# A context projection begun in the softmax tail, and the end of a linear attention with its last key chains on VectorE

## The chip, the cores and the metric

The kernel runs on one core of a Trainium2 chip. The metric is the device time of one execution in microseconds, the median of several runs.

## The reference

The input x is 4 batches of 512 tokens with 256 channels, in float32. Four residual steps follow each other, each on a layer norm of x:

```python
x = x + attn_a(layernorm(x))   # 16 heads of 16 channels, softmax over 512 keys, then ctx @ Wproj.T + bproj
x = x + ffn(layernorm(x))      # router over 8 experts, top 2; silu(silu(xr @ w1.T) @ w3.T) @ w2.T
x = x + attn_b(layernorm(x))   # 16 heads of 128: conv of 4 taps, silu, norm of q and k; S = (1-b) S + b v k'; o = S q, times gate, @ Wo
x = x + ffn(layernorm(x))
```

The expert step adds all its gated rows to the first 8 rows of x (`out.at[indices].add`), so that only a sum per expert and a small tail come after the two hidden layers.

## The kernel before

Tokens lie on the partitions in `x_tok` (16 tiles of 128 tokens). Matmuls in full precision are made of three passes with operands split into a high and a low part: ScalarE copies a bank of PSUM into the high part, VectorE subtracts it from the bank for the low part, and TensorE multiplies high x high, high x low, low x high. Each engine has its own program, and the order of all four is written out by hand; semaphores join them. A stage is a block, and at the end of a block every engine waits for all others.

The first attention goes over 8 groups (4 batches, two halves of the channels) in slots: 8 slots (chunks) for a group, 64 in all, and a lag of 6. A slot holds the row maxima of the group in hand (TensorE scores, VectorE `tensor_reduce`, L698), and the transposed scores, exponentials and context of the chunk 6 slots earlier (L441, L617, L457). So slots 64 to 69, the tail, have no maxima. Every fourth chunk a context of four head slots is copied (L624), transposed (L402) and divided by its sum into 16 columns of `ctx_tok` (L716, L718); this is done 16 times, and the 16th stands at the end of the stage, behind the last context. Scores use three banks in turn, and the context of chunk n-1 waits for all four exponentials of that chunk. In slot 66 the scores also wait for a DMA that puts the last maxima into the operands.

`project_context` (L777) is a block of its own behind it. For each batch it transposes `ctx_tok` (L799, 8 transposes), makes the high and low parts (L834, L850), multiplies with both halves of the contraction (L822, 24 matmuls in two halves) and adds to `x_tok` (L863). It also makes the high and low parts of two weights (L828, L854, L836, L870), and on the way the norm of the first group for the next stage: statistics (L83, L86), deviations on GpSimd (L96, L98), normalise (L106), transposes (L130), parts (L116, L121).

`norm_and_ffn` (L878) runs over 4 groups of 4 tiles: router (L974), two halves of the upper layer (L994), transposes of the next norms (L130), middle layer (L1006). `begun` says how many norms were counted and done ahead. The stage behind the first attention begins with (2, 1), and its GpSimd splits the head weights meanwhile (L1151 to L1177); the last stage, behind the linear attention, begins with (3, 2).

`linear_attention` (L1185) goes through 64 units (8 pairs of heads, 4 batches, 2 heads) as a software pipeline with up to 6 units in flight: projections of q and k, conv on VectorE (L1804), transposes, statistics, scales on GpSimd (L1367 to L1381, a chain of ten small instructions), normalise on ScalarE (L1705), transposes back (L1511), affine (L1721), scores (L1496), mask (L1863), sums of chunks (L1563), carry of the state (L1822), reading it out (L1578, L1581), gate (L1869), high and low parts of the gated output (L1728, L1426 on GpSimd), projection out (L1595) and addition to `x_tok` (L1846). The key chain of a unit is three instructions on GpSimd (scale L1388, shift L1404, decay L1414), and the queries' decay is a fourth (L1397). `drain()` of each engine holds what is left of the units 58 to 63 (LAST = 63), and the norms of groups 0 and 1 for the last stage. A drain thus has one order per engine:

```python
score_unit(LAST - 1, BODY - 2)                  # TensorE, before
read_state(LAST - 2, BODY - 3, LAST - 4, 0)
turn_back(LAST, 0)
sum_chunks(LAST - 1, BODY - 2)
turn_back(LAST, 1)
score_unit(LAST, BODY - 1)
ln_d.transpose(pe, 0, proj)
```

`unread(bank, n)` (L422) is n matmuls of 128x512 whose result nobody reads.

## Time and profile before

| what | us |
|---|---|
| median of 3 runs | 1172.69 (1171.26 to 1176.45) |
| the profiled execution | 1177.77 |
| its span | 1176.0 |
| TensorE busy | 1127.3 (96%) |
| VectorE busy | 932.3 (79%) |
| ScalarE busy | 773.7 (66%) |
| GpSimd busy | 635.6 (54%) |

The mean granted TensorE clock was 0.983 of full speed (2.4 GHz); where it is 0.50 the engine runs at 1.2 GHz. Rows of a timeline give start, duration, engine, line and operation; "x8" merges eight instructions. In brackets stands the idle time before the row, and what ended it. PE is TensorE, DVE is VectorE, ACT is ScalarE, POOL is GpSimd; a "q" behind a name is an engine's sequencer, which stands there where a block ended.

### The profile page before, as it was taken

The page shows a single profiled execution, that of the slowest core. Times are in us where ns is not written, and L with a number is a line of the kernel's source. Part 1 is how long each engine was busy: PE and PEld are TensorE (multiplying, and loading weights), DVE is VectorE, ACT ScalarE, POOL GpSimd, SP SyncE. Part 2 cuts the span into 40 slices and gives each one's busy share as a digit, 9 for nine tenths or more (in the row PEclk, how much of TensorE's full clock was granted, in tenths as well). Part 3 has the DMA queues.
Part 4 walks back from the last instruction along what each step waited for, and adds up shares of the span by engine and source line. Part 5 has one row for each costly group of instructions (what it writes and reads, how often), then busy time and mean ns, then how long its engine had stood idle before and what let it go on. Part 6 is the DMA issues. An engine that isn't in the chain of part 4 may idle for free. (4 is left out here: it accounts for less than half of the span.)

```text
span 1176.0 us, 22452 instructions
## 1 busy us (share of the span) xinstructions
PE 1127.3 (96%) x7559; PEld 907.9 (77%) x7559; DVE 932.3 (79%) x2126; ACT 773.7 (66%) x1535; POOL 635.6 (54%) x1077
## 2 busy tenths in 40 slices
PE   8999999987998899999999999999999999999788
PEld 7444434336666799999999999999999999999776
DVE  6988887836558888888888888888888888888762
ACT  3477677762447676767676777777777777676533
POOL 4020500000705777786777686777687777767630
PEclk9999999987999999999999999999999999999899
DMA  6333333300320112102111211211211211010020
GB/s 184 55 55 56 55 55 56 55 2 2 115 70 20 35 48 68 48 33 77 40 48 33 84 33 48 68 48 34 80 37 39 78 33 47 33 48 33 32 72 1
DMA packets 23449, 60.50 MB, mean 51 GB/s; under 512 B 3367, under 2 KB 8359, under 8 KB 22183
## 3 DMA queue, kind: packets, MB, share of 16 engines
q1 hardware_dynamic: 23335, 59.07, 18.8%
q8 instruction: 61, 1.00, 0.4%
q14 instruction: 53, 0.43, 0.1%
HBM read 44.67 MB, written 2.33 MB: 40 GB/s over the span
## 5 line engine op out<-in xcount | busy, mean ns | idle before, releaser
L1804 DVE SCALAR_TENSOR_TENSOR ln_xn<-l_proj_q,par,ln_xn 128x511 f32<-128x511 f32 (+2 forms) x192 | 142.6, 743 | 98.0 <-ACT ln_xn L1688 95.6
L698 DVE TENSOR_REDUCE a_neg_max<-a_scores 128x1 f32<-128x512 f32 x244 | 154.9, 683 | 31.2 <-PE a_scores L419 29.4
L617 ACT ACTIVATE a_probs<-a_scores_t 128x512 f32<-128x512 f32 x256 | 138.3, 600 | 59.5 <-PE a_scores_t L441 58.4
L1694 ACT ACTIVATE ln_xn<-ln_xn,par 128x512 f32<-128x512 f32 x128 | 92.6, 723 | 93.3 <-DVE ln_xn L1804 93.3
L1388 POOL TENSOR_TENSOR l_k_tok<-l_normed,k_norm 128x384 f32<-128x384 f32 x64 | 65.0, 1016 | 153.8 <-ACT l_normed L1705 151.9
L1804 DVE SCALAR_TENSOR_TENSOR ln_xn<-l_proj_k,par,ln_xn 128x511 f32<-128x511 f32 (+2 forms) x192 | 143.2, 746 | 4.5
L1705 ACT ACTIVATE l_normed<-l_turn_q,l_shift,l_scale 128x128 f32<-128x128 f32 x252 | 94.8, 457 | 22.3 <-POOL l_shift L1381 22.3
L1379 POOL TENSOR_TENSOR l_scale<-l_small,l_minus_half 128x8 f32<-128x8 f32 x64 | 105.0, 1641 | 5.0
L1705 ACT ACTIVATE l_normed<-l_turn_k,l_shift,l_scale 128x128 f32<-128x128 f32 x252 | 95.6, 480 | 0.0
L1762 ACT ACTIVATE l_gate<-l_proj_gv 128x512 f32<-128x512 f32 x64 | 38.2, 597 | 79.1 <-PE l_proj_gv L1476 79.1
L1578 PE MATMUL l_outp<-l_masked,l_values 128*128 128x128 f32 x512 | 88.6, 275 | 1.0 <-issue 1.0
L1811 DVE TENSOR_TENSOR_SCAN l_decay<-l_keep,ident 128x128 f32<-128x128 f32 x256 | 87.1, 403 | 0.0
L1426 POOL TENSOR_TENSOR l_gated_lo<-l_gated,l_gated_hi 128x512 fp32r<-128x512 f32 x64 | 83.1, 1299 | 5.1 <-ACT l_gated_hi L1728 5.1
L96 POOL TENSOR_SCALAR ln_var_eps<-ln_mean_var 128x4 f32<-128x4 f32 (+1 forms) x13 | 3.0, 230 | 148.4 <-DVE ln_mean_var L79 89.9
L441 PE MATMUL a_scores_t<-a_stack 50*128 50x512 f32 x256 | 74.9, 497 | 7.3 <-ACT a_probs L617 5.2
L1489 PE MATMUL l_proj_gv<-head_hi,xn_hi 128*128 128x256 f32 x256 | 76.5, 299 | 0.3 <-ACT l_gate L1762 0.3
L441 PEld LDWEIGHTS a_scores_t<-a_stack 50*128 50x128 f32 x256 | 28.9, 186 | 61.6 <-ACT a_probs L617 40.7
L1581 PE MATMUL l_outp<-l_q_late,l_state 128*128 128x128 f32 x384 | 74.2, 275 | 0.0
L89 POOL MEMSET ln_minus_half<- 128x4 f32 (+1 forms) x4 | 0.4, 100 | 136.1 <-POOLq L171 136.1
L1578 PEld LDWEIGHTS l_outp<-l_masked,l_values 128*128 128x128 f32 x512 | 72.6, 192 | 1.1 <-issue 1.1
L457 PE MATMUL a_ctx_acc<-a_probs,a_v_tok 128*32 128x512 f32 x512 | 70.8, 626 | 2.3 <-ACT a_probs L617 1.7
L1496 PEld LDWEIGHTS l_scores<-l_qk 128*128 128x128 f32 x512 | 67.5, 193 | 6.2 <-ACT l_qk L1721 1.3
(369 smaller groups left out, 3622.7 us busy)
## 6 DMA issues: line engine op xcount, KB each, us to landing
l_keep<-keep_rows SPq DMA_DIRECT2D x64, 448.0 KB, 3.5
a_stack<-a_dense SPq DMA_DIRECT2D x90, 128.0 KB, 4.3
head_raw<-w_heads SPq DMA_DIRECT2D x8, 1024.0 KB, 6.7
x_tok<-x SPq DMA_DIRECT2D x4, 512.0 KB, 8.3
wo_raw<-w_o SPq DMA_DIRECT2D x1, 2048.0 KB, 11.4
out<-x_tok SPq DMA_DIRECT2D x1, 1920.0 KB
a_stack<-a_max_rows_t SPq DMA_DIRECT2D x64, 4.0 KB
ctx_tok<-w_qkv SPq DMA_DIRECT2D x1, 768.0 KB, 6.8
```

What stands on the lines that cost most here:

```text
L441: pe.matmul(scores_t[q % TURNS][:], half_rows(k_stack[i], e, STACK + 2)[:, slot, t * P:(t + 1) * P], half_rows(q_stack[i], e, STACK + 2)[: ...
L617: act.activation(probs[:, n % 2, h, :], scores_t[(4 * n + h) % TURNS][:], ACT.Exp, scale=SOFT_SCALE).then_inc(probs_done, 1)
L698: dve.tensor_reduce(neg_max[:, g % 2, at:at + 1], max_bank(g, j), AX.X, ALU.max, negate=True).then_inc(max_done, 1)
L1379: pool.tensor_tensor(scale[:, i, :], small[:, 7, :], minus_half[:], ALU.pow).then_inc(scales_ready, 1)
L1426: pool.tensor_tensor(gated_lo[:, k % 4, :], gated[:], f32(gated_hi[:, k % 4, :]), ALU.subtract).then_inc(gated_lo_done, 1)
L1489: last = pe.matmul(proj_gv[:, t * PAIR:(t + 1) * PAIR], lhs, rhs, start=(j == 0), stop=(j == 3 * KD - 1))
L1578: last = pe.matmul(outp[:, tok], values[:, c % 2, t, e * DK:(e + 1) * DK], masked[:, m, tok], start=True, stop=(t == 0))
L1581: last = pe.matmul(outp[:, tok], state[:, m, t - 1, :], q_late[:, m, (t - 1) * P:t * P], start=False, stop=True)
L1694: act.activation(conv[:, w, m, :], conv[:, w, m, :], ACT.Silu, bias=par[:, h, 2 * TAPS + w:2 * TAPS + w + 1]).then_inc(act_sem[w], 1)
L1705: last = act.activation(normed[:, w, t, :], turn_bank(v, w)[:, t * P:(t + 1) * P], ACT.Identity, scale=scale[:, m, j:j + 1], bias=shift[:, ...
L1804: ins = dve.scalar_tensor_tensor(conv[:, w, m, s:], proj[w][:, 0:SEQ - s], par[:, h, tap:tap + 1], conv[:, w, m, s:], ALU.mult, ALU.add)
L1811: last = dve.tensor_tensor_scan(decay[:, tok], keep[:, r, tok], ident[:], 0.0, ALU.mult, ALU.add)
```

## The change

1. `project_context` is gone. Its work is cut into 8 parts, one for a half of the contraction and a batch. Parts 0 to 3 (the channels of the first 8 contexts) are turned in slots 64 to 67 and multiplied in slots 65 to 68; parts 4 to 7 come behind the last context. All of parts 0 to 3 use one bank, `scores[0]`, for their transposes, and two banks take the products of all 8 parts; each part is added to `x_tok` by itself. The parts of `proj_w` are made in slots 60 and 61, those of `w_in` in slots 62 and 63. The operands lie in `dense`, so no memory is added. The norm of group 0 for the next stage is done behind part 6 as before.
2. In the tail and behind it are 22 `unread` matmuls (4, 3, 4, 5, 6), in the drain of the linear attention 10 (4, 2, 4), and 4 at the head of each expert stage (both of them).
3. In `norm_and_ffn`, if one norm was done ahead, the transposes of group 1 move behind the first half of the upper layer, their high parts behind its activation, and each group's low parts come ahead of the next group's normalise. The last stage now begins with (2, 1) too.
4. In the drain of the linear attention the key chains of units 62 and 63 (but for the scaling of 62's) and the queries' decays of both are on VectorE. Norm group 1 is counted there, but no longer normalised or turned. The order on each engine is new, and the banks of the last outputs are others, so that waits for `added` fall away. ScalarE's high part of unit 60 moves ahead of the normalise of unit 62.

The core of the diff:

```diff
+            def turn_part(n):
+
+                k, b = n // NB, n % NB
+                if n == 0:
+                    pe.wait_ge(max_done, groups * tiles_per_group)
+                elif n < NB or n == PARTS - 1:
+                    pe.wait_ge(p_lo_done, min(n, NB))
+                else:
+                    pe.wait_ge(probs_done, 4 * groups * chunks)
+                pe.wait_ge(ctx_done, groups * quads // KD * (k + 1))
+                for t in range(TPB):
+                    last = pe.transpose(part_banks[n][:, t * P:(t + 1) * P], ctx_tok[:, b, t, k * P:(k + 1) * P], ident[:])
+                last.then_inc(p_turned, 1)
+
+            def project_part(n):
+
+                k = n // NB
+                pe.wait_ge(p_lo_done, n + 1)
+                if n == 0:
+                    pe.wait_ge(p_w_lo_done, 1)
+                for half in range(2):
+                    if n >= 1:
+                        pe.wait_ge(p_added, 2 * n - 1 + half)
+                    for e in range(2):
+                        tok, j = slice((2 * half + e) * P, (2 * half + e + 1) * P), 0
+                        for lhs, rhs in split_passes(ctx_hi[n % 2][:, tok], ctx_lo[n % 2][:, tok], p_w_hi[:, k, :],
+                                                     p_w_lo[:, k, :]):
+                            last = pe.matmul(acc_banks[half][:, e * D:(e + 1) * D], lhs, rhs, start=(j == 0), stop=(j == 2))
+                            j += 1
+                    last.then_inc(p_acc_done, 1)
+
             pe.wait_ge(ident_ready, 1)
...
+                        if last_max <= slot < last_max + NB:
+                            turn_part(slot - last_max)
                     else:
                         if n < 0:
                             after_context(s, c)
                         after_scores(s, c)
+                        if last_max < slot <= last_max + NB:
+                            project_part(slot - last_max - 1)
+            pe.wait_ge(ctx_done, quads * groups - 1)
+            unread(misc, 4)
             context(groups * chunks - 1)
-            pe.wait_ge(ctx_done, quads * groups - 1)
+            unread(misc, 3)
             transpose_context(quads * groups - 1)
+            unread(ctx_acc, 4)
+            for n in range(NB, PARTS):
+                turn_part(n)
+            for n in range(NB, PARTS):
+                if n == PARTS - 1:
+                    ln_b.transpose(pe, 0, norm_banks)
+                project_part(n)
+                if n == NB + 1:
+                    unread(ctx_acc, 5)
+            unread(scores_t[0], 6)
...
+            def high_part(n):
+
+                act.wait_ge(p_turned, n + 1)
+                if n >= 2:
+                    act.wait_ge(p_acc_done, 2 * (n - 1))
+                act.activation(ctx_hi[n % 2], part_banks[n][:], ACT.Copy).then_inc(p_hi_done, 1)
...
+                if slot == last_max - 4:
+                    act.wait_ge(w_loaded, 16 * len(loads))
+                    for quad in range(quads):
+                        act.wait_ge(stacked[1][quad], copies(groups - 1, quad))
+                    act.activation(p_w_hi, proj_w[:], ACT.Copy).then_inc(p_w_hi_done, 1)
+                if slot == last_max - 2:
+                    act.activation(w_in_hi[:], w_in_raw[:], ACT.Copy).then_inc(w_in_hi_done, 1)
+                if last_max <= slot < last_max + NB:
+                    high_part(slot - last_max)
             copy_context(groups * quads - 1)
+            for n in range(NB, PARTS):
...
+            def add_part(n):
+
+                for half in range(2):
+                    at = n % NB * TPB + 2 * half
+                    dve.wait_ge(p_acc_done, 2 * n + half + 1)
+                    if n == 0 and half == 0:
+                        dve.wait_ge(bias_added, 1)
+                    if n >= NB and half == 0:
+                        dve.wait_ge(p_added, 2 * (n - NB + 1))
+                    dve.tensor_tensor(x_tok[:, at:at + 2, :], acc_banks[half][:].rearrange("p (t d) -> p t d", t=2),
+                                      x_tok[:, at:at + 2, :], ALU.add).then_inc(p_added, 1)
...
+                if last_max <= slot < last_max + NB:
+                    low_part(slot - last_max)
+            normalise(groups * quads - 1)
+            low_part(NB)
+            for n in range(NB, PARTS):
+                if n + 1 < PARTS:
+                    low_part(n + 1)
+                add_part(n)
+                if n == NB:
+                    dve.wait_ge(p_added, 2 * n + 2)
+                    ln_b.statistics(dve, 0)
+                elif n == NB + 1:
+                    ln_b.normalise(dve, 0)
+                elif n == NB + 2:
+                    dve.wait_ge(p_added, 2 * n)
+                    ln_b.statistics(dve, 1)
+            ln_b.low_parts(dve, 0, norm_banks)
...
             router(0)
-            if done < 2:
-                ln.transpose(pe, 1, xt)
             for g in range(NB + 1):
                 if g < NB:
                     if g + 1 == NB:
                         turn_logits(g)
-                    for m in range(KD):
-                        upper(g, m)
+                    upper(g, 0)
+                    if g == 0 and done < 2:
+                        ln.transpose(pe, 1, xt)
+                    upper(g, 1)
...
             for g in range(done, NB):
+                if g >= done + 1 and done < 2:
+                    ln.low_parts(dve, g - 1, xt)
                 ln.normalise(dve, g)
-                if g >= done + 1:
+                if g >= done + 1 and done >= 2:
                     ln.low_parts(dve, g - 1, xt)
                 if g - done + begin < NB:
                     ln.statistics(dve, g - done + begin)
...
             def drain():
-                rows_in = 16 * NB * PAIRS
                 gated_low(LAST - 3, BODY - 4)
                 scaled_keys(LAST - 1)
                 scales(LAST, BODY - 1)
                 ln_d.deviations(pool, 0)
-                decayed_queries(LAST - 1, BODY - 2, rows_in)
-                shifted_keys(LAST - 1)
-                decayed(LAST - 1, BODY - 2)
-                scaled_keys(LAST)
-                shifted_keys(LAST)
-                decayed(LAST, BODY - 1)
                 gated_low(LAST - 2, BODY - 3)
-                decayed_queries(LAST, BODY - 1, rows_in)
-                ln_d.deviations(pool, 1)
                 gated_low(LAST - 1, BODY - 2)
                 gated_low(LAST, BODY - 1)
-                ln_d.deviations(pool, 2)
+                ln_d.deviations(pool, 1)

...
                 wait(pe, values_done, UNITS)
                 project_out(LAST - 4, BODY - 5, head)
                 score_unit(LAST - 1, BODY - 2)
+                sum_chunks(LAST - 1, BODY - 2)
                 read_state(LAST - 2, BODY - 3, LAST - 4, 0)
                 turn_back(LAST, 0)
-                sum_chunks(LAST - 1, BODY - 2)
+                unread(proj_q, 4)
+                read_state(LAST - 1, BODY - 2, 0, LAST - 1)
                 turn_back(LAST, 1)
                 score_unit(LAST, BODY - 1)
-                ln_d.transpose(pe, 0, proj)
-                read_state(LAST - 1, BODY - 2, 0, LAST - 1)
+                unread(proj_q, 2)
                 sum_chunks(LAST, BODY - 1)
                 wait(pe, added, LAST - 3)
                 project_out(LAST - 3, BODY - 4, head)
                 read_state(LAST, BODY - 1, 0, LAST)
-                wait(pe, added, LAST - 2)
                 project_out(LAST - 2, BODY - 3, head)
-                ln_d.transpose(pe, 1, proj)
+                ln_d.transpose(pe, 0, proj)
                 wait(pe, masked_done, UNITS)
                 project_out(LAST - 1, BODY - 2, head)
-                wait(pe, added, LAST - 1)
                 project_out(LAST, BODY - 1, head)
+                unread(chunks, 4)
...
                     silu(pair, k, u, 1)
+                if u == LAST:
+                    gated_high(LAST - 3, BODY - 4)
...
+            def shifted_keys(v):
+                wide = [P, LATER, DK]
+                wait(dve, k_scaled, v + 1)
+                dve.tensor_tensor(k_tok[:], k_tok[:],
+                                  k_norm[:, 1, :].unsqueeze(1).to_broadcast(wide), ALU.add).then_inc(k_shifted, 1)
...
             def drain():
                 add_out(LAST - 5, BODY - 6)
                 token_statistics(LAST, BODY - 1)
+                shifted_keys(LAST - 1)
+                decayed_keys(LAST - 1)
+                decayed_queries(LAST - 1, BODY - 2)
+                mask(LAST - 1, BODY - 2)
+                carry(LAST - 1, BODY - 2)
+                decays(LAST, BODY - 1, 16 * NB * PAIRS)
+                gate_out(LAST - 2, BODY - 3)
+                add_out(LAST - 4, BODY - 5)
                 wait(dve, added, UNITS - BODY + 2)
                 ln_d.statistics(dve, 0)
-                mask(LAST - 1, BODY - 2)
-                gate_out(LAST - 2, BODY - 3)
+                scaled_keys(LAST)
+                shifted_keys(LAST)
+                decayed_keys(LAST)
+                mask(LAST, BODY - 1)
+                decayed_queries(LAST, BODY - 1)
+                gate_out(LAST - 1, BODY - 2)
+                carry(LAST, BODY - 1)
                 ln_d.normalise(dve, 0)
-                add_out(LAST - 4, BODY - 5)
-                decays(LAST, BODY - 1, 16 * NB * PAIRS)
-                carry(LAST - 1, BODY - 2)
-                mask(LAST, BODY - 1)
-                gate_out(LAST - 1, BODY - 2)
+                gate_out(LAST, BODY - 1)
+                add_out(LAST - 3, BODY - 4)
+                add_out(LAST - 2, BODY - 3)
                 wait(dve, added, UNITS - BODY + 4)
                 ln_d.statistics(dve, 1)
-                carry(LAST, BODY - 1)
-                add_out(LAST - 3, BODY - 4)
                 ln_d.low_parts(dve, 0, proj)
-                gate_out(LAST, BODY - 1)
-                ln_d.normalise(dve, 1)
-                add_out(LAST - 2, BODY - 3)
-                wait(dve, added, UNITS - BODY + 6)
-                ln_d.statistics(dve, 2)
-                ln_d.low_parts(dve, 1, proj)
                 add_out(LAST - 1, BODY - 2)
                 add_out(LAST, BODY - 1)
```

## Rows read from the trace of the kernel before

**Rows 1.** Windows: start:end, us, busy (count) of PE, PEld, DVE, ACT, POOL, PEclk, DMA, GB/s
```profile
250.00:254.00 4.00, 2.56 (x16) 0.90 (x14) 0.00 (x0) 3.09 (x6) 0.00 (x0) 1.00 0.00 1
254.00:258.00 4.00, 3.21 (x17) 1.02 (x20) 0.00 (x0) 3.15 (x8) 0.00 (x0) 0.74 0.00 0
258.00:262.00 4.00, 4.00 (x16) 1.34 (x12) 0.37 (x2) 1.64 (x4) 0.00 (x0) 0.50 0.00 0
294.00:296.00 2.00, 2.00 (x8) 1.29 (x7) 1.91 (x9) 0.59 (x1) 0.00 (x0) 0.50 0.87 283
1110.00:1112.00 2.00, 1.12 (x4) 0.72 (x4) 2.00 (x3) 1.41 (x5) 1.88 (x2) 0.50 0.00 0
```

**Rows 2.** TensorE's timeline in the softmax tail: start us, us, engine line op [idle before]
```profile
246.74 0.28 PE L396 MATMUL a_misc<-ident,a_max_parts 128*32 128x128 f32 x1
...
248.63 1.06 PE L457 MATMUL a_ctx_acc<-a_probs,a_v_tok 128*32 128x512 f32 x8
...
249.62 0.50 PE L441 MATMUL a_scores_t<-a_stack 50*128 50x512 f32 x2
...
266.05 1.94 PE L457 MATMUL a_ctx_acc<-a_probs,a_v_tok 128*32 128x512 f32 x8 [1.17 <-ACT a_probs L617]
```

**Rows 3.** ScalarE's timeline in the softmax tail
```profile
244.60 2.07 ACT L617 ACTIVATE a_probs<-a_scores_t 128x512 f32<-128x512 f32 x4 [0.65 <-PE a_scores_t L441]
```

**Rows 4.** VectorE's timeline at the end of the softmax tail
```profile
270.20 0.42 DVE L718 TENSOR_TENSOR ctx_tok<-a_misc,a_rden 128x256 f32<-128x256 f32 x1
```

**Rows 5.** TensorE's timeline in the projection's stage and behind it
```profile
276.76 0.28 PE L822 MATMUL p_acc<-p_w_hi,p_ctx_hi 128*128 128x256 f32 x1
...
278.56 1.03 PE L799 MATMUL p_turned<-ident,ctx_tok 128*128 128x128 f32 x8
...
292.93 0.40 PE L974 MATMUL f_sums_b<-xn_hi,w_in_hi 128*8 128x512 f32 x1 [2.25 <-PEq L779]
```

**Rows 6.** VectorE's timeline in the projection's stage
```profile
271.60 0.69 DVE L854 TENSOR_TENSOR p_w_lo<-proj_w,p_w_hi 128x512 fp32r<-128x512 f32 x1 [0.97 <-ACT p_w_hi L828]
...
279.48 1.41 DVE L83 BATCH_NORM_STATS2 ln_stats<-x_tok 128x6 f32<-128x256 f32 x4
...
282.25 1.28 DVE L863 TENSOR_TENSOR x_tok<-p_acc,x_tok 128x512 f32<-128x512 f32 x2
...
284.07 1.38 DVE L106 TENSOR_SCALAR ln_xn<-x_tok,ln_mean_var,ln_rstd 128x256 f32<-128x256 f32 x4
```

**Rows 7.** GpSimd's timeline in the projection's stage
```profile
281.65 1.04 POOL L98 TENSOR_TENSOR ln_rstd<-ln_var_eps,ln_minus_half 128x4 f32<-128x4 f32 x1
```

**Rows 8.** TensorE's timeline in the first expert stage
```profile
300.02 0.40 PE L974 MATMUL f_sums_b<-xn_hi,w_in_hi 128*8 128x512 f32 x1 [0.26 <-DVE xn_lo L121]
...
307.35 0.40 PE L974 MATMUL f_sums_b<-xn_hi,w_in_hi 128*8 128x512 f32 x1 [1.62 <-DVE xn_lo L121]
```

**Rows 9.** VectorE's timeline in the first expert stage
```profile
303.03 3.07 DVE L106 TENSOR_SCALAR ln_xn<-x_tok,ln_mean_var,ln_rstd 128x256 f32<-128x256 f32 x4 [1.47 <-POOL ln_rstd L98]
...
312.03 3.52 DVE L1094 TENSOR_TENSOR beta_lo<-beta_w,beta_hi 128x32 fp32r<-128x32 f32 x1
```

**Rows 10.** GpSimd's timeline in the first expert stage
```profile
311.90 3.61 POOL L1175 TENSOR_SCALAR wo_hi<-wo_raw 128x4096 fp32r<-128x4096 f32 x1
```

**Rows 11.** GpSimd's timeline in the linear attention's drain
```profile
1103.84 1.00 POOL L1388 TENSOR_TENSOR l_k_tok<-l_normed,k_norm 128x384 f32<-128x384 f32 x1
...
1106.56 1.64 POOL L1379 TENSOR_TENSOR l_scale<-l_small,l_minus_half 128x8 f32<-128x8 f32 x1
...
1128.10 1.35 POOL L1426 TENSOR_TENSOR l_gated_lo<-l_gated,l_gated_hi 128x512 fp32r<-128x512 f32 x1 [1.57 <-ACT l_gated_hi L1728]
```

**Rows 12.** ScalarE's timeline in the drain
```profile
1108.51 1.50 ACT L1705 ACTIVATE l_normed<-l_proj_q,l_shift,l_scale 128x128 f32<-128x128 f32 x4 [4.67 <-POOL l_shift L1381]
```

**Rows 13.** TensorE's timeline in the drain and behind it
```profile
1110.07 1.12 PE L1511 MATMUL l_turn_q<-ident,l_normed 128*128 128x128 f32 x4 [3.43 <-ACT l_normed L1705]
...
1134.61 0.39 PE L974 MATMUL f_sums_d<-xn_hi,w_in_hi 128*8 128x512 f32 x1 [1.69 <-PEq L1204]
```

160 lines of the change are left out of this document (58 added, 102 removed).

## The prediction

> **What bounds the kernel now.** I read the busy times first, then the windows of the span, then the timelines of the two places that the change touches. TensorE is busy for 96% of the span, so a gain must come from where it isn't, or where it is busy at half its clock. The windows show two such stretches. In the softmax tail it works for 2.56 of 4 us at 250 to 254, and then the granted clock goes from 1.00 to 0.74 to 0.50, that is from 2.4 to 1.2 GHz [rows 1]. The same matmuls of the context take 1.06 us at 248.6 and 1.94 us at 266.0 [rows 2]. Full clock is back at 276.8, in the middle of the projection, where a matmul of 256 columns follows the one before it by 0.12 us and eight transposes take 1.03 us [rows 5]. In the drain of the linear attention TensorE waits 3.43 us for ScalarE's normalise, which itself waited 4.67 us for GpSimd's scales [rows 12, 13], and it runs at 0.50 from there [rows 1]. After both the next stage starts late: the first router matmul stands at 292.93 with 2.25 us idle before it, and at 1134.61 with 1.69 us [rows 5, 13]. After the idle time of 2.25 us the clock fell again, 0.50 at 294 to 296 [rows 1].
>
> **Softmax tail, slots 64 to 69.** Before, from the last transpose of maxima at 246.74 to the end of the last context's division at 270.62 it is 23.9 us [rows 2, 4]. New work for TensorE in slots 65 to 67: two pairs of scores at 0.35 to 0.5, together 0.7, a context 1.0 from its start to that of the scores behind it [rows 2], four transposes 0.5, twelve matmuls at 0.12 make 1.4 [rows 5], together 3.6 us. ScalarE has four exponentials, 2.1 us [rows 3], and a high part of 0.6, so 2.7. But parts 0 to 3 share one bank, and so there is a ring: transposes 0.5, the slot's second pair of scores 0.5 to its first exponential, two exponentials 1.1, high part 0.6, low part 0.65, hand-overs 0.3, together 3.7 us, a little more than TensorE's own work. Slot 64 ends at 248.4, four slots of 3.7 make 263.2, slot 69 with scores and context 1.8 makes 265.0. Then the last exponentials, the context at full clock, the copy, transposes and the division: 1.8, 1.0, 0.7, 0.6 and 0.8, which makes 269.9. That is 0.7 us early. The 7 unread matmuls stand in the waits for the exponentials and the copy. The weights' parts in slots 60 to 63 are 1.3 us on ScalarE and 0.69 twice on VectorE [rows 6]; both have idle time there, so between 0 and 2.7 us; I take 0.6, for VectorE paces the maxima. Sum of the tail: about 0 (bounds: 2 us gained, 5 lost). The DMA of the maxima that slot 66 waits for is covered by the new work.
>
> **The projection behind the last context.** Before: 270.62 to 292.93, 22.3 us [rows 4, 5]. New, from the division's end: the block's end and the weights' first parts are gone. Four unread matmuls lie beside the division. First part turned at 0.6, high part 1.2, low part 1.9, products to 3.5. From there VectorE is the chain: adding 1.28 a part [rows 6], statistics 1.6 (1.41 begins, the aggregates follow), low parts 0.6 each, normalise 1.38 [rows 6], with GpSimd's 1.04 [rows 7] beside an addition. From 1.9: low part of 5 beside the products, first addition 2.9 to 4.2, statistics 5.8, low part 6.4, addition 7.6, normalise 9.0, low part 9.6, addition 10.8, statistics 12.4, addition 13.6, low parts of the norm 14.8, end of the block 15.1. TensorE has 16 transposes and 48 matmuls, half of before, and fits in. Gain 22.3 - 15.1 = 7.2; I take 7 (bounds 5 and 9).
>
> **The first expert stage.** Four unread matmuls cost 0.9 us, as nothing is waited for. Router(1) then waits for the low parts of group 1: 0.9 + 1.4 router + 1.4 upper + 0.9 transposes, high parts behind the activation and its table load, low parts: 6.9 us from the start, against 300.02 - 292.93 = 7.1 with a stretch at half clock [rows 8, 1]. Router(2) waited 1.62 us for low parts that stood behind a normalise of 3.07 us [rows 8, 9]; they now stand ahead of it, and this stall goes; late next are the transposes of group 3, by at most 0.5. Whether the clock falls is open: TensorE's gap is 2.2 us now as well. Held: 2.0 gained, fallen: 1.0. I take 1.5 (bounds 2 and -1).
>
> **The drain.** The time from the scales' end S (ScalarE's normalise begins, 1108.51 [rows 12]) to the router at 1134.61 [rows 13] is 26.1 us. New, in us after S and at full clock (where no row is named, the steps at the pace that they have in the 600 us of steady state before: turning back 0.5, scores 1.0, sum of chunks 0.7, reading the state 1.5, and 0.6 to 0.7 for an instruction of ScalarE or VectorE over 512 columns, as the additions' [rows 6]): normalise of q and k to 2.8 (1.4 each); turn back q 2.0, four unread 2.9, reading unit 62's state 4.5, turn back k 5.0, affine 5.9, scores 7.0, mask 7.7, queries 8.2, gate of 62 8.9, carry 9.5, with the sum of chunks to 8.2 and a projection out to 9.7 beside it; reading unit 63 to 11.2. VectorE's normalise stands ahead of the gate of 63 and meets GpSimd's low part, 2.3 instead of 1.4: 11.8, gate 12.5, high part 13.1, low part on GpSimd 1.35 [rows 11] to 14.5, two projections out at 24 x 0.12 to 17.4, last addition and unread 18.3, block's end 18.7. That is 7.4 less. The key chain of 63 on VectorE (3 x 0.55, from 0.69 for 512 columns and 0.42 for 256 [rows 6, 4], against 1.00 on GpSimd [rows 11]) ends at 5.2, before the scores, so it costs nothing; if the scores were not the later ones, it would cost 1.7. S itself: GpSimd's scales begin 1.0 us earlier, since unit 60's high and low parts came earlier, and end 0.3 to 1.0 earlier, but the three instructions for unit 62 on VectorE fall in the midst of them.
>
> A row decides what that costs. In the expert stage a VectorE subtraction of 128x32 with both inputs in SBUF took 3.52 us while GpSimd ran one instruction of 3.61 us [rows 9, 10], so the two don't run side by side. The Trainium skill, page "SBUF — State Buffer", section "SBUF: two separate sides", says the same as a rule: the pair of ports that both engines share is taken for a whole instruction by a VectorE operation with two inputs in SBUF against a GpSimd operation that reads SBUF. By that rule, as by the row, moving keys to VectorE is no free relief for the engine that makes the scales.
>
> By the row, the chain of scales is held up by 0 to 3 x 0.55 = 1.7 us; I take 0.8 and S unchanged. Then the last stage pays: four unread matmuls 0.9, the transposes of group 1 0.9, and a wait of 0.6 for their parts, 2.4. Drain and last stage: 7.4 - 0.5 (GpSimd held up beyond the early start) - 2.4 = 4.5 gained (bounds 7 gained, 1 lost).
>
> **Sum.** 0 + 7 + 1.5 + 4.5 = 13.0 us. The profiled execution took 1177.77 (span 1176.0 and 1.8 around it), so 1164.8 for it; it was 5.1 above the median of 1172.69. From the median: 1159.7. Within 0.5% is 5.9 us, about what a measurement can tell.
>
> **Rivals.** (a) The ring in the tail is slower than 3.7 us a slot: the high part stands behind the slot's exponentials, and each slot's scores wait for banks. For: ScalarE's exponentials often wait for scores in the tail, 0.65 us before one group [rows 3]. Against: all steps were counted. At 5.0 a slot it costs 4 x 1.3 = 5 us: 1165.
> (b) The drain gives nothing: GpSimd's scales wait for VectorE, TensorE is then idle for 2 to 2.5 us before the turn back of q, and its clock falls as it did behind 3.43 and 2.25 us of idle time, doubling some 4 us of work. For: those two rows [rows 5, 13]; against: 1.69 us of idle time brought no fall. 0.8 more for S and 4 for the clock: 1164.5.
> (c) Slower than before: the clock falls in slot 64 or 65 already and doesn't come back up to the end of the projection. Then 3.6 us of TensorE's work a slot becomes 7.2, four slots and a half give 16, and behind the last context some 4 more: 20 - 13 = 7 over, 1180. For: in this tail it did fall, and the projection's matmuls up to 276 ran at half [rows 1, 5]. Against: it fell behind a stretch with 1.4 of 4 us idle, which now has the parts in it. It decides from about 13 us of work at half clock on.
> (d) (a) and (b) together, or a covered stall in both, which ends within 0.5%: 1168.
>
> **Chances.** Forecast 0.58, (a) 0.13, (b) 0.13, (c) 0.06, (d) 0.10. The forecast's own range is 1155 to 1165; with (a), (b) and (d) 1154 to 1170. Faster by over 0.5% (under 1166.8): the forecast and nearly all of (a) and (b), 0.82; the same: (d) and the rest, 0.12; slower: 0.06.
>
> **What would show it.** Right: no block between the tail and the projection; granted clock near 1.00 from 246 to the first expert stage; slots 65 to 68 of 3.5 to 3.9 us; the last division near 270; from there to the router about 15; router(2) without a wait; the drain from S to the last stage's router about 19 us, and S within 1 us of before. Wrong: 0.50 in any window from 250 to 285, slots of over 4.5 us, ScalarE's normalise of unit 63 later than before relative to the last step, or the last stage longer by more than 3 us.

## The result, and the profile after

The changed kernel takes 1168.41 us (median of 13 runs, 1167.14 to 1170.89) against 1172.70 (13 runs, 1171.14 to 1179.90): ratio 0.996, 95% interval 0.9949 to 0.9972, so 4.3 us less by the medians, where 13.0 were forecast. The time lies outside the forecast's own range (1155 to 1165) and inside the one that takes in the rivals (1154 to 1170); the gain is a third of the forecast. The profiled execution took 1167.14, the lowest of the 13, and its span is 1165.3. Medians here and below leave out three runs in a slow state: two of the kernel before (1390.21 and 2754.50 us) and one of no_unread (1249.68).

The table splits the span of the two profiled executions at the points that the prediction used: the last transpose of maxima (slot 64), the last division, the next block's first matmul on TensorE, the linear attention's first, the scales' end S, and the last stage's first.

| stretch, us | before | after | difference | forecast |
|---|---|---|---|---|
| up to the transpose of slot 64 | 246.74 | 247.17 | +0.4 | 0 |
| tail, to the last division | 23.88 | 24.50 | +0.6 | 0 |
| projection, to the first expert stage | 22.31 | 15.48 | -6.8 | -7 |
| first expert stage | 41.67 | 39.95 | -1.7 | -1.5 |
| linear attention up to S | 773.91 | 773.65 | -0.3 | +0.5 |
| drain behind S | 26.10 | 20.66 | -5.4 | -7.4 |
| last stage | 41.39 | 43.89 | +2.5 | +2.4 |
| span | 1176.0 | 1165.3 | -10.7 | -13.0 |

By these two executions the forecast was 2.3 us off; by the medians it was 8.7 off. The profiled execution of before stands 5.1 us above its median and that of after 1.3 below, which are the 6.4 us between the two answers. The experiments must say where in the span they lie.

The windows of after (columns as in [rows 1]):

```profile
250.00:254.00 4.00, 3.85 (x32) 2.44 (x28) 1.22 (x2) 2.60 (x6) 0.00 (x0) 1.00 0.01 2
254.00:258.00 4.00, 4.00 (x32) 2.43 (x28) 1.33 (x3) 3.07 (x7) 0.00 (x0) 1.00 0.00 0
258.00:262.00 4.00, 4.00 (x32) 2.37 (x31) 2.30 (x4) 2.63 (x5) 0.00 (x0) 1.00 0.00 0
...
294.00:296.00 2.00, 1.89 (x11) 0.84 (x12) 2.00 (x8) 0.30 (x1) 0.00 (x0) 1.00 1.03 433
...
1104.00:1108.00 4.00, 3.49 (x20) 3.16 (x18) 1.36 (x3) 0.80 (x2) 1.14 (x1) 0.68 0.00 0
```

The clock stays at 1.00 through the tail, where it was 0.74 and 0.50 [rows 1], and TensorE is busy nearly all the time, not 2.56 of 4 us. At 294 it is 1.00 as well. In the drain it still falls, to 0.68.

One slot of TensorE's timeline in the tail of after, and ScalarE's exponentials in it:

```profile
249.50 1.07 PE L471 MATMUL a_ctx_acc<-a_probs,a_v_tok 128*32 128x512 f32 x8
250.72 0.66 PE L571 MATMUL a_scores<-ident,ctx_tok 128*128 128x128 f32 x4 [0.15 <-DVE a_dense L805]
251.30 0.50 PE L455 MATMUL a_scores_t<-a_stack 50*128 50x512 f32 x2
251.74 1.70 PE L587 MATMUL a_scores<-a_dense 128*128 128x256 f32 x12
...
253.79 1.06 PE L471 MATMUL a_ctx_acc<-a_probs,a_v_tok 128*32 128x512 f32 x8
```

```profile
251.83 1.09 ACT L678 ACTIVATE a_probs<-a_scores_t 128x512 f32<-128x512 f32 x2 [0.92 <-PE a_scores_t L455]
```

From context to context the slot takes 4.29 us, the next ones 4.07 (the contexts start at 257.86, 261.94 and 265.81). TensorE does not wait within it but for 0.15 us: context 1.0, transposes 0.58, scores 0.43 twice, twelve matmuls 1.63. It is ScalarE that waits, 0.92 us, for scores that stand behind the twelve matmuls.

VectorE from the last division on, and TensorE at the start of the first expert stage:

```profile
271.25 0.42 DVE L798 TENSOR_TENSOR ctx_tok<-a_misc,a_rden 128x256 f32<-128x256 f32 x1
...
278.50 1.28 DVE L816 TENSOR_TENSOR x_tok<-a_scores,x_tok 128x512 f32<-128x512 f32 x2
```

```profile
287.15 1.17 PE L1031 MATMUL f_up_b<-w_in_hi 128*128 128x512 f32 x4 [1.69 <-PEq L171]
...
294.11 0.39 PE L994 MATMUL f_sums_b<-xn_hi,w_in_hi 128*8 128x512 f32 x1 [0.77 <-DVE xn_lo L121]
...
299.63 0.39 PE L994 MATMUL f_sums_b<-xn_hi,w_in_hi 128*8 128x512 f32 x1
```

The additions take 1.28 us, the statistics 1.40 and the normalise 1.37, as before [rows 6]. The router of group 1 comes 6.96 us after the start of the stage, that of group 2 without the wait of 1.62 us [rows 8].

The drain of after on ScalarE, TensorE and VectorE:

```profile
1100.75 1.51 ACT L1724 ACTIVATE l_normed<-l_proj_q,l_shift,l_scale 128x128 f32<-128x128 f32 x4 [2.23 <-POOL l_shift L1405]
```

```profile
1097.30 0.91 PE L1578 MATMUL l_chunks<-l_values,l_k_tok 128*128 128x128 f32 x6 [0.15 <-issue]
...
1102.31 0.66 PE L1526 MATMUL l_turn_q<-ident,l_normed 128*128 128x128 f32 x4 [2.54 <-ACT l_normed L1724]
1102.72 1.71 PE L1667 MATMUL l_proj_q<-wo_hi 128*128 128x512 f32 x4
...
1121.41 1.16 PE L1031 MATMUL f_up_d<-w_in_hi 128*128 128x512 f32 x4 [0.30 <-PEq L1228]
```

```profile
1111.98 2.36 DVE L106 TENSOR_SCALAR ln_xn<-x_tok,ln_mean_var,ln_rstd 128x256 f32<-128x256 f32 x4
```

ScalarE's wait for the scales is 2.23 us instead of 4.67 [rows 12], but not because the scales come earlier: the copy of unit 62's state, 0.28 us at 1098.24, now stands in the midst of it and itself waits 2.59 us. TensorE waits 2.54 us instead of 3.43 [rows 13], since the sum of unit 62's chunks (1097.30) now stands ahead of S. Even so the clock falls behind this wait: the four unread matmuls behind the turn back of q take 1.51 us up to the next row at 1104.23, and reading unit 62's state 2.66, up to 1106.89.

S itself comes later. The last conv instruction of VectorE ends 10.6 to 10.7 us before S in the four profiled executions with the old drain, and 11.3 to 11.4 us before it in the eight with the new one. What differs between them on VectorE is the scans of the decays, in before and in after:

```profile
1100.26 1.36 DVE L1811 TENSOR_TENSOR_SCAN l_decay<-l_keep,ident 128x128 f32<-128x128 f32 x4
```

```profile
1091.81 2.11 DVE L1830 TENSOR_TENSOR_SCAN l_decay<-l_keep,ident 128x128 f32<-128x128 f32 x4
```

In after, GpSimd's low part of unit 60 runs from 1091.40 to 1092.69, earlier than before, and the scans that begin beside it take 0.75 us longer. VectorE's normalise at 1111.98 takes 2.36 us beside GpSimd's low part (1112.17 to 1113.55); 2.3 were assumed.

### The profile page after: what moved, and what is told of

Read it like the earlier page. It is cut to its first block and busy times, and to the rows that moved or that the text cites. A ratio compares the mean times of both kernels' runs of the same rounds, so it can differ in the third digit from the quotient of the medians.

```text
span 1165.3 us, 22548 instructions
## 1 busy us (share of the span) xinstructions
PE 1126.4 (97%) x7599; PEld 908.6 (78%) x7599; DVE 939.7 (81%) x2141; ACT 774.3 (66%) x1535; POOL 629.9 (54%) x1070
## 5 line engine op out<-in xcount | busy, mean ns | idle before, releaser
L1724 ACT ACTIVATE l_normed<-l_turn_q,l_shift,l_scale 128x128 f32<-128x128 f32 x252 | 95.0, 458 | 21.6 <-POOL l_shift L1405 21.5
L1504 PE MATMUL l_proj_gv<-head_lo,xn_hi 128*128 128x256 f32 x256 | 71.1, 278 | 0.0
L1504 PE MATMUL l_proj_gv<-head_hi,xn_lo 128*128 128x256 f32 x256 | 70.9, 277 | 0.0
```

The lines of the kernel that those rows point to most:

```text
L1504: last = pe.matmul(proj_gv[:, t * PAIR:(t + 1) * PAIR], lhs, rhs, start=(j == 0), stop=(j == 3 * KD - 1))
L1724: last = act.activation(normed[:, w, t, :], turn_bank(v, w)[:, t * P:(t + 1) * P], ACT.Identity, scale=scale[:, m, j:j + 1], bias=shift[:, ...
```

## The experiments

Every kernel stood beside runs of the kernel before on the same chip. "Before" is the median of those runs.

| kernel | us | before | ratio, 95% interval |
|---|---|---|---|
| before_again | 1173.11 | 1173.13 | 0.9994 (0.998 to 1.0008) |
| a_only | 1171.17 | 1173.13 | 0.9982 (0.9969 to 0.9995) |
| b_only | 1171.35 | 1173.13 | 0.9985 (0.9968 to 1.0002) |
| no_unread | 1166.28 | 1173.13 | 0.994 (0.9922 to 0.9958) |
| after_again | 1168.83 | 1173.86 | 0.9956 (0.9938 to 0.9974) |
| parts_late | 1169.99 | 1173.86 | 0.9966 (0.9954 to 0.9978) |
| spread | 1166.05 | 1173.86 | 0.9928 (0.9909 to 0.9948) |
| no_drain_fill | 1166.52 | 1173.86 | 0.993 (0.9911 to 0.9949) |
| spread_no_fill | 1165.31 | 1173.14 | 0.9928 (0.9914 to 0.9942) |
| before_fill | 1173.71 | 1173.14 | 1.0001 (0.999 to 1.0012) |

And the stretches of their profiled executions, in us, as in the table above:

| kernel | to slot 64 | tail | projection | expert | to S | drain | last | span |
|---|---|---|---|---|---|---|---|---|
| before_again | 247.06 | 19.24 | 21.61 | 41.67 | 774.93 | 26.68 | 41.41 | 1172.6 |
| a_only | 245.93 | 24.50 | 15.46 | 39.97 | 775.36 | 27.08 | 41.40 | 1169.7 |
| b_only | 246.64 | 19.23 | 20.83 | 41.66 | 775.59 | 20.63 | 43.92 | 1168.5 |
| no_unread | 247.00 | 24.98 | 17.39 | 40.32 | 775.59 | 19.38 | 42.94 | 1167.6 |
| after_again | 246.10 | 24.44 | 15.46 | 39.94 | 776.36 | 20.64 | 43.96 | 1166.9 |
| parts_late | 246.40 | 19.16 | 23.26 | 39.96 | 774.22 | 20.67 | 43.93 | 1167.6 |
| spread | 247.18 | 23.21 | 15.47 | 39.94 | 775.13 | 20.67 | 43.90 | 1165.5 |
| no_drain_fill | 246.43 | 24.44 | 15.48 | 39.93 | 776.15 | 19.24 | 42.93 | 1164.6 |
| spread_no_fill | 245.87 | 23.20 | 15.49 | 39.97 | 777.43 | 19.59 | 42.95 | 1164.5 |
| before_fill | 245.88 | 19.55 | 20.95 | 41.63 | 777.60 | 26.60 | 41.39 | 1173.6 |

**before_again**, the kernel before, unchanged.

> The kernel before, unchanged, for the spread of its executions and a second profile. Theory 1 (the forecast's base was a slow execution): in the profiled execution of before, at 1177.8 us, TensorE's clock fell in places where it does not fall in most others, so the times lie in groups, near 1171.3 and from 1174 to 1178, and the mean granted clock is higher in the faster group (0.983 was that of the profiled one). A profile near 1171 then shows full clock in the tail at 256 to 276 or in the drain behind S. Theory 2 (the change itself loses time in executions other than the profiled one): before's times show no relation to its mean clock, and a profile near 1171 has the same windows at 0.50 as the one at 1177.8. Ratio to before 1.000 either way.

Its windows, the last context on TensorE and the last division on VectorE:

```profile
254.00:258.00 4.00, 3.00 (x17) 1.00 (x21) 0.00 (x0) 3.35 (x7) 0.00 (x0) 1.00 0.00 0
258.00:262.00 4.00, 3.88 (x26) 1.30 (x18) 0.68 (x2) 2.83 (x7) 0.00 (x0) 1.00 0.00 0
...
266.00:270.00 4.00, 3.37 (x16) 3.21 (x16) 1.83 (x4) 2.10 (x4) 0.10 (x1) 0.59 0.01 2
```

```profile
263.05 1.06 PE L457 MATMUL a_ctx_acc<-a_probs,a_v_tok 128*32 128x512 f32 x8 [1.16 <-ACT a_probs L617]
```

```profile
265.88 0.42 DVE L718 TENSOR_TENSOR ctx_tok<-a_misc,a_rden 128x256 f32<-128x256 f32 x1
```

The last context takes 1.06 us, not 1.94 [rows 2], and the tail 19.24 us, not 23.88 [rows 2, 4]. In the tail and the projection the clock falls only behind the division, 0.59 at 266 to 270. So the half clock of [rows 1] was not a property of the kernel but of that execution: at 250 to 254 TensorE is busy for 2.62 of 4 us here and for 2.56 there, the program is the same, and only there did the clock fall behind it. The times also go with the mean clock, from 1171.88 us at 0.994 to 1174.85 at 0.988, as Theory 1 said.

**a_only**: the tail, the projection and the first expert stage of after; drain and last stage of before.

```diff
...
-        norm_and_ffn(nc, semaphore, "d", ffn, xn_hi, xn_lo, ident, x_tok, norm_tiles, ln_d, (2, 1), out=out)
+        norm_and_ffn(nc, semaphore, "d", ffn, xn_hi, xn_lo, ident, x_tok, norm_tiles, ln_d, (NB - 1, NB - 2), out=out)
```

> Only the part at the softmax tail and the first expert stage: projection without its stage, 22 unread matmuls, the 4 at the head of the first expert stage and its new order; linear attention and last stage as before. By the two profiled executions this part gave 1.1 lost up to the last division, 6.8 and 1.7 gained behind it, 7.5 us in all. Theory 1: the fall of the clock that is missing in most executions of before is that of the drain, so this part holds its 7.5 us: 1165.2, and b_only is slower than before. Rival: the missing fall is that of the tail (256 to 276), and this part gives only 3 us: 1169.7.

**b_only**: the other half, drain and last stage of after on the tail, projection and first expert stage of before. The cut is against after.

```diff
...
-            softmax_attention(nc, semaphore, x, w_qkv, w_stack, loads, bias_rows, x_tok, xn_hi, xn_lo, ident, ctx_tok, norm_tiles, proj_w,
-                              (w_in_raw, *ffn[:2]), ln_b)
+            softmax_attention(nc, semaphore, x, w_qkv, w_stack, loads, bias_rows, x_tok, xn_hi, xn_lo, ident, ctx_tok, norm_tiles)
+            project_context(nc, semaphore, proj_w, ctx_tok, ident, x_tok, ln_b, (w_in_raw, *ffn[:2]))
```

> Only the linear attention's drain and the last expert stage changed: key chains on VectorE, new orders, 10 unread matmuls, 4 at the head of the last stage, which begins with one norm less. By the two profiled executions: 5.4 gained from S to the last stage, 2.5 lost in it, 2.9 us in all. Theory 1: before's drain mostly runs at full clock, where its 26.1 us are about 22, so this part loses 1 to 2 us: 1174. Rival: it holds its 2.9 us: 1169.8.

a_only gains 2.0 us and b_only 1.8 (b_only's interval takes in no gain), together 3.8 where both at once gain 4.3: within the noise the halves add up, and the forecast failed in both, by more in a (8.5 forecast) than in b (4.5). Of what was expected before the runs, the rivals (1169.7 and 1169.8, the missing fall is that of the tail) are nearer than Theory 1 (1165.2 and 1174), and both are 1.5 us too low. With the tail of 19.2 us and the projection of before_again, a's stretches give +5.3, -6.2 and -1.7. Its drain, with the orders of before, shows what b removes, on TensorE and on GpSimd:

```profile
1105.85 1.62 PE L1587 MATMUL l_chunks<-l_values,l_k_tok 128*128 128x128 f32 x6 [2.42 <-issue]
```

```profile
1104.76 0.99 POOL L1438 TENSOR_TENSOR l_k_tok<-l_k_tok,l_decay 128x384 f32<-128x384 f32 x1 [0.17 <-POOL l_k_tok L1428]
```

Behind the turn back of q TensorE waits another 2.42 us, until GpSimd's decay of unit 62's keys ends at 1105.75, and then runs the sum of chunks at half clock (the windows 1104 to 1112 have 0.50). With part b VectorE makes these keys ahead of S, the sum stands there too, and this second wait is gone.

**no_unread**: after without all its 40 added unread matmuls.

```diff
-            unread(misc, 4)
...
-            for _ in range(4):
-                pe.matmul(up[0][:], w_in_hi[:, 0, 0:P], w_in_hi[:, :, 0:D], start=True, stop=True)
...
-                unread(proj_q, 4)
...
```

> The changed kernel without its 40 unread matmuls (22 at the tail and behind it, 10 in the drain, 4 at the head of each expert stage). If they hold the clock: a lower mean clock than 0.994, falls to 0.50 behind the tail and in the drain, and 2 to 4 us more than the changed kernel, 1171 to 1172. If they don't: the 8 at the heads of the stages lie on the path, 0.9 us each stage, and it is 1.5 to 2 us faster, 1166.5.

```profile
270.00:274.00 4.00, 2.98 (x13) 2.61 (x14) 0.79 (x3) 0.66 (x2) 0.00 (x0) 0.52 0.00 0
274.00:278.00 4.00, 3.85 (x22) 3.68 (x20) 2.13 (x4) 0.71 (x2) 0.00 (x0) 0.63 0.00 0
```

Without them the clock falls behind the last context, to 0.52 and 0.63 where after has 1.00, and tail and projection take 2.4 us more. Drain and last stage take 2.2 us less. So those of the tail and the projection hold the clock, and those of the drain and the last stage only delay. By the stretches the kernel should be 0.6 us slower than after; by the medians it is 2.1 faster than after's 1168.41, on another chip and with 5 runs, and the intervals of the two ratios overlap. That is not resolved.

**after_again**, the changed kernel once more.

> The changed kernel once more, for a second profiled execution and as the level that the three other variants are read against. Theory 1 (in the tail TensorE's own work sets the slots now, 4.07 us each at full clock, where ScalarE's exponentials set 2.7 before, so the tail lost 5.3 us against an execution of before with full clock): the tail from the last transpose of maxima to the last division takes 24.5 us again (24.2 to 24.8), the stretch behind it to the first expert stage 15.5, time 1168.4 (1167 to 1171), 4 to 5 us under before. Rival (the 24.5 us were one execution's chance, as the 23.9 of before were): the tail differs by over 1 us from 24.5.

The tail takes 24.44 us and the time is 1168.83: Theory 1 holds. after_again and before_again can be compared stretch by stretch, since in both the clock also fell at about 350 to 366 and at 390 us (it fell at 324 to 332 too in after_again alone): up to slot 64 -1.0, tail +5.2, projection -6.2, expert stage -1.7, up to S +1.4, drain -6.0, last stage +2.6, together -5.7, near the -5.0 of the medians of that chip.

**parts_late**: no part in the tail.

```diff
-                        if last_max <= slot < last_max + NB:
-                            turn_part(slot - last_max)
...
-                        if last_max < slot <= last_max + NB:
-                            project_part(slot - last_max - 1)
...
-            for n in range(NB, PARTS):
+            for n in range(NB):
                 turn_part(n)
-            for n in range(NB, PARTS):
+            for n in range(PARTS):
...
+                if n < NB:
+                    turn_part(n + NB)
...
```

> All eight parts of the context's projection stand behind the last division, none in slots 64 to 69; the weights' parts, the unread matmuls and everything behind stay as in the changed kernel. Theory 1 (TensorE's work for four parts, 4 x (0.58 + 1.63) = 8.8 us, fills 3 to 4 us of idle time and costs the other 5 in the tail): tail 19.2 to 19.6 us instead of 24.5, stretch behind the division about 15.5 + 4 additions of 1.28 = 20.6 on VectorE's chain, together 40, so the time is the same as the changed kernel's within 1 us: 1167.5 to 1169.5. Rival (the parts beside the exponentials were nearly free, as forecast, and the loss against the forecast lies elsewhere): tail 23 or more without them as well, sum 44, time 1172.

```profile
265.14 0.42 DVE L793 TENSOR_TENSOR ctx_tok<-a_misc,a_rden 128x256 f32<-128x256 f32 x1
...
268.62 1.41 DVE L811 TENSOR_TENSOR x_tok<-a_scores,x_tok 128x512 f32<-128x512 f32 x2 [0.47 <-PE a_scores L586]
...
276.61 1.35 DVE L811 TENSOR_TENSOR x_tok<-a_scores,x_tok 128x512 f32<-128x512 f32 x2
```

```profile
288.82 1.16 PE L1022 MATMUL f_up_b<-w_in_hi 128*128 128x512 f32 x4 [1.68 <-PEq L171]
```

The tail is 19.16 us. So the four parts cost 5.3 us there. Behind the last division they cost 7.8 (23.26 against 15.46), not the 5.1 expected. That had only the additions of 1.28 us, but VectorE also makes each part's low part, 0.6 us: from the first addition (268.62) to the fifth (276.61) it takes 8.0 us with hardly a wait, 2.0 a part. The way from the division to the first addition is no longer than in after (3.1 us against 3.2). Tail and projection together are 42.4 against 39.9. The time, 1169.99, is 0.5 above the expected range. By the profiles the parts' place in the tail thus brings 2.5 us; of the medians 1.2 (1169.99 against 1168.83).

**spread**: halves of a part, one a slot.

```diff
+        turn_slot = {64: 0, 66: 1, 68: 2, 69: 3}
+        half_slot = {65: (0, 0), 66: (0, 1), 67: (1, 0), 68: (1, 1), 69: (2, 0)}
...
-                        if last_max < slot <= last_max + NB:
-                            project_part(slot - last_max - 1)
-            pe.wait_ge(ctx_done, quads * groups - 1)
-            unread(misc, 4)
+                        if slot in half_slot:
+                            project_part(half_slot[slot][0], (half_slot[slot][1],))
+            project_part(2, (1,))
             context(groups * chunks - 1)
-            unread(misc, 3)
+            project_part(3, (0,))
+            pe.wait_ge(p_lo_done, 4)
             transpose_context(quads * groups - 1)
-            unread(ctx_acc, 4)
+            project_part(3, (1,))
...
```

> The first four parts are projected by halves of a part, one half in each of the slots 65 to 69, part 2's second half ahead of the last context and part 3's halves in place of the unread matmuls behind it; all else as in the changed kernel. Theory 1 (TensorE's work sets the slots, so what counts is work per slot against the 2.7 us of the exponentials): 1.86 for scores and context, 0.58 x 4 + 0.82 x 5 over six slots add 1.07, so 2.9 to 3.0 a slot instead of 4.07; tail 20.5 to 21.5 us, stretch behind it 15.5, time 1165 (1164 to 1166.5). Rival (the ring through the one bank for turning, with high part, low part and hand-overs, sets the slots): they stay at 3.7 or more and the tail at 23.5 or more, 1167.5.

```profile
252.26 1.07 PE L473 MATMUL a_ctx_acc<-a_probs,a_v_tok 128*32 128x512 f32 x8
...
254.28 0.98 PE L589 MATMUL a_scores<-a_dense 128*128 128x256 f32 x6
...
256.05 1.07 PE L473 MATMUL a_ctx_acc<-a_probs,a_v_tok 128*32 128x512 f32 x8 [0.36 <-issue]
...
257.90 0.95 PE L589 MATMUL a_scores<-a_dense 128*128 128x256 f32 x6 [0.36 <-DVE x_tok L818]
```

```profile
269.97 0.42 DVE L800 TENSOR_TENSOR ctx_tok<-a_misc,a_rden 128x256 f32<-128x256 f32 x1
```

The slots take 2.8 to 3.8 us, 3.4 on the mean, so they are no longer 4.07; but the tail is 23.21 us, 1.2 less than after_again and 2 more than Theory 1 said. TensorE's work sets these slots too. The expectation spread four groups of transposes and five halves over six slots, 1.07 us each. In the five slots from the context at 249.51 to that at 266.57 there are six halves at 0.9 us, not 0.82, and three groups of transposes, 7.1 us and so 1.4 a slot; with 1.86 for scores and context that is 3.3 of the 3.4 measured. Part 3's halves behind the last context cost 0.6 more there: from its start to the division's end it is 3.8 us against 3.2 in after. The ring is not it: of TensorE's waits only 0.36 us in these slots is for an addition. The time is 1166.05, 2.8 less than after_again, and no run of the one lies among those of the other.

**no_drain_fill**: after without the ten unread matmuls of the drain and the four at the last stage's head.

```diff
-                unread(proj_q, 4)
...
-                unread(proj_q, 2)
...
-                unread(chunks, 4)
...
-            for _ in range(4):
+            for _ in range(4 if tag == "b" else 0):
```

> The changed kernel without the ten unread matmuls in the drain and the four at the head of the last stage; those of the softmax tail, of the projection and of the first expert stage stay. Theory (TensorE's wait behind the scales is over before they begin, so they only delay, and the clock falls ahead of them anyway): drain from the scales' end 19.4 us instead of 20.7, last stage 42.9 instead of 43.9, the rest as in the changed kernel, together 2.2 less: 1166.2 (1165 to 1167). Rival (they hold the clock up for what follows): granted clock 0.50 in more of the drain, and no gain or a loss of up to 2: 1168 to 1170.

```profile
1104.00:1108.00 4.00, 3.92 (x22) 3.52 (x22) 2.68 (x10) 2.04 (x6) 1.64 (x2) 0.64 0.00 0
```

```profile
1121.67 0.39 PE L994 MATMUL f_sums_d<-xn_hi,w_in_hi 128*8 128x512 f32 x1 [1.05 <-PEq L1228]
```

1166.52, 2.3 us less than after_again, and again no run of the one lies among those of the other; drain 19.24, last stage 42.93, as expected. The clock falls with them (0.68) and without (0.64): they begin when the wait is over.

**spread_no_fill**: the edits of spread and of no_drain_fill together.

> The kernel with parts projected by halves in the tail, and without the unread matmuls of the drain and of the last stage's head: the two variants that gained, together. If they are independent (the one lies before 286 us, the other behind 1100): tail 23.2 us, stretch behind it 15.5, drain 19.2, last stage 42.9, time 1168.8 - 2.8 - 2.3 = 1163.7 (1162.5 to 1165), 9 to 10 us under before. Rival (the clock ties them, less work held at full clock in the one place costs it in the other): 1165 or more.

1165.31, 7.8 us less than before and the lowest median of all kernels run, but its ratio is that of spread alone. 1163.7 was expected if the two are independent, 1165 or more if not. The profiled stretches add up but for 0.35 us in the drain; up to S the profiled execution takes 2.3 us more than that of spread, with a fall of the clock at 356 to 364. Whether the two are really not additive, or six runs each are too few, is open.

**before_fill**: the kernel before with 20 unread matmuls in the idle time of its tail.

```diff
                         after_scores(s, c)
+                        if slot >= groups * chunks + 1:
+                            pe.wait_ge(max_done, groups * tiles_per_group)
+                            unread(scores[0], 2)
+            unread(scores[0], 3)
             context(groups * chunks - 1)
...
```

> The kernel before, with 20 unread matmuls of 512 columns in TensorE's idle time in its softmax tail (two in each of slots 65 to 69, three ahead of the last context, three ahead of its transposes, four beside the last division), and nothing else changed. Theory (the spread of before's times from 1171 to 1180, and the 4.7 us by which its first profiled execution was longer, come from whether the granted clock falls in this tail): the clock is at 1.00 to 270 in the profile, the tail takes 19.2 to 20.0 us, and all times lie close together, 1170.5 to 1173, with a median of 1171 to 1172. Rival (the spread comes from elsewhere in the span): times up to 1177 and over as before, the same median as before within 1.

```profile
258.00:262.00 4.00, 4.00 (x25) 2.04 (x23) 0.68 (x2) 3.19 (x6) 0.00 (x0) 1.00 0.00 0
...
266.00:270.00 4.00, 2.77 (x24) 2.56 (x25) 2.85 (x5) 3.10 (x6) 0.00 (x0) 1.00 0.01 2
```

The clock holds through the tail and behind it. Of 63 runs of the kernel before in these experiments 8 took 1176.7 us or more, with mean clocks of 0.982 to 0.987; of the 12 runs of before_fill none took more than 1175.7. Twelve runs alone don't show much: at 8 in 63, none in 12 comes by chance about one time in five. Over all kernels it is clearer. Of the 100 runs whose kernel has the tail of before without these matmuls, 11 lie more than 3.5 us above the median of their series; of the 74 whose kernel has a changed or filled tail (no_unread aside), none does, and the furthest is 2.5 above. So the tail (with what lies right behind it) explains the slowest executions of before; where in the span those others were slow, no profile shows. The median is the same as before, 1171 to 1172 was wrong, and times still spread over 3.4 us: most executions never had the fall that the forecast counted on removing.

## Why the prediction was wrong

**The tail's base, the step that failed.** "Before, from the last transpose of maxima at 246.74 to the end of the last context's division at 270.62 it is 23.9 us", and then "That is 0.7 us early." The 23.9 us hold 4.6 us of half clock that most executions don't have: the tail takes 19.24 in before_again and 19.23 in b_only. The prediction even saw that this execution "was 5.1 above the median", and took the gain from the median all the same. A gain that comes from a stretch in which only the profiled execution was slow can't be taken from the median. With the right base the prediction's own tail of 23.2 us (269.9 - 246.74) is 3.9 more than before, not 0, and the projection saves 5.4 to 6.2, not 7: 1159.7 + 3.9 + 0.8 to 1.6 = 1164.4 to 1165.2. The 0.6 us for the weights' parts don't show: up to slot 64 the four executions with the old tail take 246.6 us on the mean and the eight others 246.5.

**The tail's size.** The slots were forecast at 3.7 us, set by a ring through one bank, with 3.6 for TensorE. They take 4.07, and TensorE's own work sets them: twelve matmuls 1.63 instead of 1.4, pairs of scores 0.43 instead of 0.35, transposes 0.58 instead of 0.5. Two of the three could be read in the tail of before, where these instructions stand in the same company:

```profile
246.95 0.51 PE L441 MATMUL a_scores_t<-a_stack 50*128 50x512 f32 x2
247.39 0.66 PE L402 MATMUL a_misc<-ident,a_ctx_t 128*128 128x128 f32 x4
```

From start to start the pair takes 0.44 us and the four transposes 0.59, as the next row begins at 247.98. The 1.4 for twelve matmuls came from a long row of one shape. So the tail is 24.5 us instead of 23.2, 1.3 more. The matmuls fill TensorE's idle time, but behind slot 66 there was only 0.8 us of it a slot at full clock: ScalarE's exponentials paced the slots at 2.7 us, with 1.9 of TensorE's work in them.

**The projection.** 15.1 from the division on was forecast, 15.5 measured in every kernel with it; the chain through VectorE held to 0.4 us. Its base too had half clock in it: 21.6 in before_again, where the clock fell behind the division, and 20.8 in b_only, where it didn't, instead of 22.3. So the saving is 6.2 or 5.4 us.

**The first expert stage.** 1.5 forecast, 1.7 measured, and router(2) waits for nothing. Right.

**The drain.** 18.7 us was forecast with every step at full clock, 20.66 measured. 1.8 of the 2.0 arise in two steps that ran at half clock in after: the first four unread matmuls, 1.51 us instead of 0.9, and reading unit 62's state behind them, 2.66 instead of 1.5. The steps behind keep about the forecast's distances. Without the ten unread matmuls the drain takes 19.24, so they cost 1.4 us and hold nothing. Rival (b)'s mechanism, an idle time of 2 to 2.5 us and a fall behind it, did come (2.54 and 0.68), but it came in the kernel before as well, so most of the gain stayed. The saving is 6.0 us between after_again and before_again, 1.4 less than forecast.

S was forecast 0.5 us later. The whole stretch up to S can't tell, as it differs by up to 4 us between executions with the clock. From the last conv on it is about 0.7 us later in every execution with part b. That is the sign that the prediction gave for being wrong, ScalarE's normalise of unit 63 later than before, but in size it is the term that it had counted. It came by another way: the scales' chain is longer (4.4 to 4.5 us instead of 3.7) but begins so much earlier that it makes nothing later, and the loss is in VectorE's scans beside GpSimd's earlier low part, which the prediction did not have.

**The last stage.** +2.4 forecast, +2.5 measured. 1.0 of it is the four unread matmuls at its head.

**The sum again.** 1164.4 to 1165.2 with the right base, 1.3 for the slots, 1.4 for the drain and 0.2 for S make 1167.3 to 1168.1; the medians say 1168.4. The rest is within what 13 runs each can tell (the interval of the ratio is 2.7 us wide).

**The rivals.** (a) had the tail too slow, but by the ring and by 5.0 us a slot; the measured cause is TensorE's work. (c) did not happen: the clock is 1.00 from 246 to the end of the first expert stage. (d), 1168, has the right time for a reason that it did not name.

## What to carry to other kernels

When the profiled execution is slower than the median, find where in its trace the surplus lies before subtracting anything: if it lies where the change is, the change removes what a typical execution doesn't have. Work put beside an engine that paces a stretch is free only up to the idle time at full clock; cost it by what is left in a slot, and with shapes alternating, not from a row of one shape. Here unread matmuls helped ahead of a wait or inside it (2.4 us in tail and projection) and only delayed behind one (1.4 us in the drain). And a wait that got shorter on one engine says nothing by itself: ScalarE's went from 4.67 to 2.23 us while what it waits for came 0.7 us later; measure from a point that the change leaves alone.
